# Routed expert pairs with copied weights as the stationary operand, in one decoder-layer kernel on Trainium2

## What is computed

```
g = jax.nn.silu(jnp.einsum('th,efh->tef', x, w1_e))
u = jnp.einsum('th,efh->tef', x, w3_e)
routed = jnp.einsum('tef,ehf,te->th', g * u, w2_e, combine)
```

## Time and profile before

| | |
|---|---|
| median of 3 runs | 1096.35 us (1094.07 to 1097.78) |
| span of the profiled execution, first to last instruction | 1075.3 us |
| median less span | 21.05 us |
| TensorE matmul busy | 975.3 us, 91% |
| VectorE busy | 773.2 us, 72% |
| ScalarE busy | 685.0 us, 64% |
| GpSimd busy | 632.8 us, 59% |

### The profile page before, as it was taken

How to read it: one execution, slowest core, us unless ns; L and a number is a source line. 1 busy time by engine, 2 the same in 40 slices (tenths; PEclk the granted TensorE clock), 3 DMA queues, 4 the chain that set the end, 5 groups by cost and what they waited for, 6 DMA issues and landing times.

```text
span 1075.3 us, 21635 instructions
## 1 busy us (share of the span) xinstructions
PE 975.3 (91%) x6502; PEld 750.0 (70%) x6502; DVE 773.2 (72%) x1634; ACT 685.0 (64%) x2182; POOL 632.8 (59%) x683
## 2 busy tenths in 40 slices
PE   4668999999999999998899999989999999999996
PEld 2446667677677676776667767657788888888775
DVE  2287889889898898899988989875442222455687
ACT  0168767767767677776676776866456555566533
POOL 5664456765767567665676665312555555566654
PEclk7789999999999999999999999999999999999999
DMA  9704333353344431112211111012444544688765
GB/s 259 237 18 146 96 105 110 117 185 116 127 142 136 141 109 49 52 59 85 78 49 52 59 40 52 33 57 78 138 130 147 156 152 132 210 260 284 247 208 183
DMA packets 97872, 135.38 MB, mean 126 GB/s; under 512 B 11203, under 2 KB 83554, under 8 KB 97761
## 3 DMA queue, kind: packets, MB, share of 16 engines
q1 hardware_dynamic: 84704, 101.53, 30.7%
q0 software_dynamic: 13056, 32.47, 8.2%
HBM read 61.91 MB, written 76.23 MB: 128 GB/s over the span
## 4 chain that ended last, share of the span: by engine, by line
PE 46%; DVE 33%; issue 8%; ACT 4%; POOL 4%; DMA 2%; SPq 2%; DVEq 0%; POOLq 0%; ACTq 0%
DVE Sc L1315 7%; PE four L834 6%; PE bT L834 5%; PE four L875 5%; PE bT L589 5%; PE bM L575 4%; DVE wkv L1292 4%; DVE nmx L1317 4%; PE four L760 4%; PE bO L796 3%; PE bU L726 3%; DVE st L1230 3%; PE bM L582 2%; DMA yg<-Yt 2%; ACT Sc L1055 2%
## 5 line engine op out<-in xcount | busy, mean ns | idle before, releaser
L1055 ACT ACTIVATE Sc<-Sc,nmx 128x256 f32<-128x256 f32 x512 | 253.6, 501 | 8.2 <-DVE nmx L1317 8.2
L1063 ACT ACTIVATE PT<-bT 128x512 f32<-128x512 f32 x256 | 151.7, 592 | 136.5 <-PE bT L589 135.4
L1718 POOL DMA_INDIRECT Yt<-PT,dests x150 | 150.0, 1000 | 100.5 <-ACT PT L1134 70.0
L589 PE MATMUL bT<-idn,Sc 128*128 128x128 f32 x1024 | 161.5, 280 | 6.3 <-ACT PT L1063 5.3
L589 PEld LDWEIGHTS bT<-idn,Sc 128*128 128x128 f32 x1024 | 114.4, 141 | 71.8 <-issue 57.3
L1315 DVE TENSOR_SCALAR Sc<-four 128x1024 f32<-128x1024 f32 x128 | 155.3, 1213 | 9.5 <-PE four L760 6.1
L1317 DVE TENSOR_REDUCE nmx<-Sc 128x4 f32<-128x1024 f32 x128 | 156.2, 1220 | 4.4
L1701 POOL DMA_INDIRECT Xs<-x,slots x120 | 121.2, 1010 | 35.2 <-issue 18.3
L575 PE MATMUL bM<-mix,Wp 128*128 128x256 f32 x384 | 100.6, 408 | 35.8 <-DVE wkv L1287 20.7
L575 PEld LDWEIGHTS bM<-mix,Wp 128*128 128x128 f32 x384 | 73.5, 202 | 50.5 <-issue 38.4
L1055 ACT ACTIVATION_READ_ACCUMULATOR Sc<-Sc,nmx 128x1 f32 x512 | 99.0, 193 | 0.0
(11 more groups left out here) (220 smaller groups left out, 2024.8 us busy)
## 6 DMA issues: line engine op xcount, KB each, us to landing
Xs<-yg SPq DMA_DIRECT2D x16, 1768.0 KB, 7.9
xb<-Xs SPq DMA_DIRECT2D x152, 136.0 KB, 2.1
yg<-Yt SPq DMA_DIRECT2D x27, 512.0 KB
W<-w SPq DMA_DIRECT2D x4, 1152.0 KB, 11.2
xTs<-xT SPq DMA_DIRECT2D x16, 256.0 KB, 3.0
x<-x SPq DMA_DIRECT2D x16, 256.0 KB, 3.0
Base<-stg SPq DMA_DIRECT2D x15, 256.0 KB, 2.3
out<-acc SPq DMA_DIRECT2D x15, 256.0 KB, 4.1
```

What stands on the lines that cost most here:

```text
L589: last = pe.transpose(dst[:, j, t * P:(t + 1) * P], src[:, t, j * P:(j + 1) * P], idn[:, :])
L1055: last = fn(Sc[:, n % 3, m, t, :], Sc[:, n % 3, m, t, :], ACT.Exp, bias=nmx[:, n % 3, m, t:t + 1], accum_out=rs[:, s % 2, t, h:h + 1])
L1063: fn(flat(PT[:, h % RING]), bT[:, :], ACT.Copy).then_inc(a_pt.sem, 1)
L1718: pool.indirect_dma_start(Yt, bass.IndirectOffsetOnAxis(ap=dests[:, i % IDS, b:b + 1], axis=0), y_rows(i)[:, b, :], None, bounds_check=SPA ...
```

## The change

Gate and up weights become the stationary operand of a routed pair. A stationary operand at a register's address isn't used: VectorE first copies the weights of each block (128 x 512 elements) into half of `QT` (`stage`), with the offset that it loads into a register itself. The product then comes out with hidden features on the partitions, as `down` needs it, so the two turns, ScalarE's `copy_hidden` and their waits go for routed pairs. `down` moves one slot earlier (i - 2), and `copy_y` and `scatter` too (i - 3). The dense units are as before.

```
+            def stage(i, b):
+                if b == 0:
+                    dve.wait_ge(d_rows.sem, d_rows.at(PAIR_EPOCH[i].k))
...
+                elif i <= FIRST + 1:
+                    dve.wait_ge(p_gu.sem, p_gu.at(i - 2))
+                else:
+                    dve.wait_ge(p_slot.sem, slot_done(i - 2))
+                w = dve.value_load(w_of[0:1, 2 * i + b:2 * i + b + 1], min_val=2 * 2 * F, max_val=(BLK - 1) * 2 * F)
+                dve.tensor_copy(QT[:, i % 2, b], W13[:, :, :, :, :].rearrange("p j c n f -> p j (c n f)")[:, :, bass.ds(w, 2 * F)]).then_inc(d_stage.sem, 1)
...
             def tail(u):
                 i = u - START
+                if i + 1 < ROUTED:
+                    stage(i + 1, 0)
+                    stage(i + 1, 1)
                 if FIRST < i <= UNITS:
                     hidden(i - 1)
...
                 for b in range(2):
-                    for j in range(ND):
-                        if i < ROUTED:
-                            wj = W13[:, j].rearrange("p c n f -> p (c n f)")
-                            last = mm(cols(gu_bank(i))[:, b, :], xbT[:, i % 2, j, b, :], wj[:, bass.ds(w[b], 2 * F)], start=(j == 0), stop=(j == ND - 1))
-                        else:
+                    if i < ROUTED:
+                        for n in range(2):
+                            for j in range(ND):
+                                last = mm(cols(gu_bank(i))[:, b, n * P:(n + 1) * P], QT[:, i % 2, b, j, n * F:(n + 1) * F], xbT[:, i % 2, j, b, :],
+                                          start=(j == 0), stop=(j == ND - 1))
...
-                if late(i - 2) and i - 2 < UNITS:
+                if late(i - 2) and i - 2 < ROUTED:
+                    last = down(i - 2, weights.pop(i - 2))
+                if ROUTED <= i - 2 < UNITS:
                     last = turn_hidden(i - 2)
-                if late(i - 3):
-                    last = down(i - 3, weights.pop(i - 3, None))
+                if ROUTED <= i - 3 < UNITS:
+                    last = down_dense(i - 3)
...
-                    if late(i - 3) and i - 3 < UNITS:
+                    if ROUTED <= i - 3 < UNITS:
                         copy_hidden(i - 3)
-                    if late(i - 4) and i - 4 < ROUTED:
-                        copy_y(i - 4)
+                    if late(i - 3) and i - 3 < ROUTED:
+                        copy_y(i - 3)
```

More of the change, by code:

```diff
@@ L385, in decoder_layer @@
         d_dense = event("d_dense")
+        d_stage = event("d_stage", 2)
         d_last = event("d_last")
@@ L842, in turn_hidden, with down_dense @@
             def turn_hidden(i):
-                dst = bC
                 pe.wait_ge(d_t2.sem, d_t2.at(i))
[L845 to L850, removed]
-                else:
[L852 to L855, removed]
+                if i == ROUTED:
+                    pe.wait_ge(a_y.sem, a_y.at(ROUTED - 1))
+                else:
+                    pe.wait_ge(a_h.sem, a_h.at(i - 1 - ROUTED))
                 for b in range(2):
-                    last = pe.transpose(dst[:, b * P:(b + 1) * P], hid(i)[:, b, :], idn[:, :])
-                if not late(i):
-                    last.then_inc(p_h.sem, 1)
+                    last = pe.transpose(bS[:, 0, b * P:(b + 1) * P], hid(i)[:, b, :], idn[:, :])
                 return last
             def down(i, w):
-                pe.wait_ge(a_h.sem, a_h.at(i))
-                w2f = W2[:, :, :].rearrange("p c d -> p (c d)")
+                pe.wait_ge(d_t2.sem, d_t2.at(i))
+                if not late(i):
+                    pe.wait_ge(a_xb.sem, a_xb.at(i + 1))
+                elif i <= FIRST:
+                    pe.wait_ge(d_clip.sem, d_clip.at(PAIRS - 1))
+                else:
+                    pe.wait_ge(a_y.sem, a_y.at(i - 2))
+                w2f = W2[:, :, :].rearrange("p c d -> p (c d)")
+                for b in range(2):
+                    last = mm(y_bank(i)[:, b * D:(b + 1) * D], hid(i)[:, b, :], w2f[:, bass.ds(w[b], D)], start=True, stop=True)
+                if not late(i):
+                    last.then_inc(p_y.sem, 1)
+                return last
+            def down_dense(i):
+                pe.wait_ge(a_h.sem, a_h.at(i - ROUTED))
                 if i == ROUTED:
@@ L868, in down @@
                     pe.wait_ge(d_acc.sem, d_acc.at(DENSE))
-                if late(i - 1) and i < ROUTED:
-                    pe.wait_ge(a_y.sem, a_y.at(i - 1))
                 for b in range(2):
[L872 to L879, removed]
+                    last = mm((bO, bU)[b][:, 0:D], turned(i)[:, b, :], W2[:, 2 + i - ROUTED, :], start=(i == ROUTED), stop=(i == UNITS - 1))
                 return last
@@ L925, in slot @@
                         load_weights(0, 1)
-                    gate_up(i, weights[i])
+                    gate_up(i)
                     load_weights(i + 1, 0)
@@ L962, in tail @@
                 if i < UNITS:
-                    last = gate_up(i, weights.get(i))
+                    last = gate_up(i)
                 load_weights(i + 1, 0)
@@ L1110, in copy_hidden, with copy_y @@
             def copy_hidden(i):
+                act.wait_ge(p_slot.sem, slot_done(i + 2))
+                fn(turned(i), bS[:, 0, 0:2 * P].rearrange("p (b t) -> p b t", b=2), ACT.Copy).then_inc(a_h.sem, 1)
+            def copy_y(i):
                 if late(i):
                     act.wait_ge(p_slot.sem, slot_done(i + 2))
[L1113 to L1123, removed]
                     if not late(i - 1):
@@ L1764, in tail @@
                     scatter(i - 2)
-                if late(i - 4) and i - 4 < ROUTED:
-                    scatter(i - 4)
+                if late(i - 3) and i - 3 < ROUTED:
+                    scatter(i - 3)
                 if u in WIDE_AT:
```

31 lines of the change are left out of this document (15 added, 16 removed).

## The result

The changed kernel takes 1136.97 us (median of 4 runs, 1135.16 to 1139.67), the kernel before 1097.07 beside it: 1.037 times as long, 95% interval 1.034 to 1.041. Forecast were 1101, with a range from 1087 to 1120. The direction was the one that the forecast gave a chance of 0.54; the size was not.

What follows compares the result with a forecast made beforehand. Two close limits were taken to bound a slot: TensorE's own work, 3.25 us, and a loop through ScalarE and VectorE, 3.41. Terms -8.9 + 12.4 + 2 - 0.5 = +5.0 us gave 1101 us, range 1087 to 1120.

Steps and rivals of the forecast that it cites:

- The direction: Whole kernel: slower than before by over 0.3%, given a chance of 0.54.
- pairs 2 to 14: Stretch before 801: TensorE saves 2.2 us, stages on the path cost 4.3; taken as +2 us.
- middle, 37 slots: Pairs running alone: stage just hidden beside the tanh, slot 3.40 to 3.16 us, -8.9 us.
- combines, 24 slots: Slots beside combines: stage not hidden behind a combine on VectorE, 4.0 us a slot, +12.4 us.
- the whole stage: VectorE, each pair: two register loads and two copies take 1.8 us, the second load beside the first copy.
- The forecast of 28.7 for seven slots: Combine stretch: two slots of 5.4 us behind moments, two of 4.2 without, three of 3.16.
- The frame: Whole kernel: profiled 1075.3 us becomes 1080.3, and with 21 us around it 1101.3.
- +5.0: Whole kernel: sum of all stretches, 5.0 us slower.
- Loads wait for copies: Rival, VectorE: stage takes 2.2 us or more; +20 us, 1117 us; chance 0.17 (with copies waiting for GpSimd).
- The queue absorbs the stages: Rival, VectorE: loads run ahead of the combine, stage costs 1.1 us or less; -5 us, 1091 us; chance 0.25.
- DMA issues slowed by the copies: Rival, GpSimd: copies shut out DMA issues, 3.4 us a pair, no middle gain; +14 us, 1110 us; chance 0.05.
- Narrow records are paced by more than 0.11: Rival, TensorE's gate and up: records at 0.14 us, slot 3.55 us; 1119 us in all; chance 0.05.

Runs made afterwards that it cites:

- after_again: The changed kernel, unchanged, run again on another chip, without late signals, where the kernel before takes 1084.6 us: 1097.8 us, ratio 1.013.
- before: The kernel before the change, in the profiled execution that the prediction read: span 1075.3 us.
- after: The changed kernel as first measured and traced, against the kernel before: 1137.0 us, ratio 1.037.
- before_again: The kernel before, no edit, profiled again beside the first follow-up runs: 1091.3 us (one run).
- own_wait: The changed kernel, but a slot's gate and up also wait for TensorE's own signal of the slot before: 1114.0 us, ratio 1.018.
- stage_fixed: The changed kernel, but stage copies one fixed expert's weights, so VectorE loads no register: 1073.5 us, ratio 0.988 to the kernel before.
- the first two sets of runs: Variants of the changed kernel in record width, stage, turns, waits, PSUM bank and registers, beside the kernel before: 1080.5 to 1138.5 us.
- the other three sets: Variants with fixed addresses or moved waits and loads; the changed kernel again with stage variants; stage's loads one slot ahead: 1061.3 to 1102.3 us.

## Why the prediction was wrong

Stretch by stretch, in us: the forecast, the chip without late signals (after_again less the trace of before) and the chips with them (after less before_again):

| stretch | forecast | without | with |
|---|---|---|---|
| pairs 2 to 14 | +2 | 56.6 - 52.2 = +4.4 | 64.0 - 62.0 = +2.0 |
| middle, 37 slots | -8.9 | 118.4 - 126.1 = -7.7 | 150.3 - 126.3 = +24.1 |
| combines, 24 slots | +12.4 (with a 25th) | 105.7 - 83.9 = +21.8 | 104.2 - 85.8 = +18.4 |

Each difference is one execution less one other. The trace of before is a quick one: its span and 1.8 us make 1077.1, where the median beside after_again is 1084.6. So 7 us of the 20.1 between these two spans are not the change's, and which stretch holds them isn't known.

**The step that failed** is the middle stretch's -8.9. It let the signal of `down` reach ScalarE and VectorE at its record's end, as in the earlier trace rows. On the chip that gave the result it is 1.9 us late in every second slot. The late signals add up to 32.5 us, and the stretch takes 31.9 more than after_again's 118.4: +24.1 instead of a gain. The rest of that step held: where signals are in time the slot is 3.20, forecast 3.16 to 3.19. That the long delays of this stretch need TensorE to run on ahead of its signal is shown by own_wait (-23 us). Why the changed order has late signals there and the kernel before has none (3.41 a slot on either kind of chip), and which part of a chip or its set-up makes them, is open. That a wait in mid slot frees them wasn't tried on a chip that has them.

**The second failed size** is the combine slot. The parts of the stage were right: load to copy 0.63 to 0.75 (forecast 0.7), copy 0.43 (0.41), the whole stage 1.82 (1.8). The forecast of 28.7 for seven slots became 5.91 + 4.82 + 3.10 + 5.54 + 4.82 + 3.09 + 3.20 = 30.5, but not from the terms forecast. Over the 24 slots of after_again, the seven behind moments take 5.4 to 6.8 each, 41.5 instead of 7 x 5.4 = 37.8. Combines without moments were given 4.2 and are mostly hidden, so that about 7 us were forecast too much. The six slots of 4.8 are at the lower clock behind TensorE's idling, 9.9 us more than at 3.16, and no term of the sum was for the clock. That the seven-slot sum is off by 1.8 only is in part luck: one error made up for much of the other. With the 25th slot, as forecast, the stretch gains 110.0 - 86.8 = 23.2 us instead of 12.4.

**The frame** was wrong. 1101 was reached as 1080 plus 21 us "around" the span. In the runs here with both on record, about 1.8 us lie around a span. The rest of the 21 is the difference between the execution that was traced and those that were timed. That these were on two kinds of chip is inferred: the chip of the trace isn't on record, but its update records are as complete as on the chips without late signals, and none of its signals is late. What the trace could forecast was the kernel on a chip like its own: +5.0 there, where it measured 1097.8 - 1084.6 = +13.1. The direction held on both kinds of chip. Where signals are late, more than half of the loss has a cause that the forecast did not know.

**The rivals.** "Loads wait for copies" fell: the second load runs beside the first copy. "The queue absorbs the stages" fell in the combines: the first load started at 949.32, beside the last operation of the combine and no sooner. "DMA issues slowed by the copies" fell as a bound: GpSimd's issue has a median of 985 ns among 152 copies (0.98 in the earlier trace rows). The Trainium skill (SBUF — State Buffer, SBUF: two separate sides) has the rule that such a copy locks GpSimd out; that row does not show it. A small effect isn't excluded: the mean of an issue is 1.00 us in before and in after_again, and 1.06 in stage_fixed, where the two copies follow each other at once. "Narrow records are paced by more than 0.11" fell: 1.78 / 16 = 0.111.

## What to carry to other kernels

Cost a wait on another engine's behalf twice: for its length, and for what it can do to TensorE's clock in the slot behind it. Here an idle of 1.0 us cost 1.0; idles of 2.2 to 3.5 cost their length and in many slots, not in all, 1.7 more. A register load on a compute engine's queue took 0.63 us from the signal to the copy, more than the 0.43 of the copy of 128 x 512 elements that it serves. Loading one slot ahead took back part of that, and still held the next operation up by 0.65 behind a combine. And compare a span with the time of the same execution before taking a trace for the kernel that was timed.

## What the runs showed that was not expected

TensorE's signal can reach its waiters 1.9 us behind the record that gives it (4.7 in before_again), while records behind it run on and the next signal is in time. It does so in the trace of after and in those of the first two sets of runs, and in none of the other three sets, which ran on other chips, nor in the trace of before. The split is sharp: each of the nine traces with late signals has 72 to 104 signals of TensorE that are over 0.1 us late, before_again 72 of them, most by 0.1 to 0.4 in the attention; the other eleven traces have none. In the traces of the former about three in ten records of semaphore updates are missing (9,732 with after, 13,706 with after_again, same program). That is not what makes a signal look late: the late updates are on record, and where one is missing, as for most of `p_slot` in own_wait, "issue" stands as releaser. The Trainium skill (NOTIFIC — the notification-queue block, Overflow: three behaviours, one of which stalls the engine) says that the block which takes such records can hold back what feeds it; whether that is what delays the signals, no run here shows. Every run has a span and a clock on record, so none tells whether signals are late when nothing is recorded.

The time of the kernel before differs by 1.0 to 1.5% between the two kinds of chip (1095.1 to 1097.1, and 1081.3 to 1084.6), as much as the change's own effect on the better one. Of the 14.2 us between the spans of before_again and before, 9.8 lie between pairs 2 and 14, where the signal 4.7 us late and the lower clock behind it stand.
